# Drawing the first group's patch weights out of all experts by one-hot matmuls, with identity matmuls and four score banks in that group

## What is computed

```python
x = x + _L0_conv_ref(_gn(x), Wg, bg, Wexp, bexp)
x = x + _L1_conv_ref(_gn(x), w_route, b_route, w_experts)
x = x + _L2_conv_ref(_gn(x), codebook)
x = x + _L3_conv_ref(_gn(x), w_grid, b_grid, w_conv)
```

```python
feat = patched.mean(axis=(2, 3))
logits = feat @ Wg + bg
probs = jax.nn.softmax(logits, axis=-1)
routing = jax.nn.one_hot(jnp.argmax(logits, axis=-1), E) * probs
```

## Time and profile before

| | |
|---|---|
| median of 3 runs | 1939.35 us (1932.0 to 1942.69) |
| the profiled execution | 1936.7 us |
| its span, first to last instruction | 1934.9 us |
| TensorE busy | 1606.0 us, 83% |
| VectorE busy | 1449.0 us, 75% |
| ACT busy | 1099.4 us, 57% |
| POOL busy | 1210.8 us, 63% |
| mean granted TensorE clock | 0.933 |

### The profile page before, as it was taken

The page is one execution under the profiler, slowest core; times in us unless marked ns, Lnnn a source line. Parts: engine busy times, 40 slices in busy tenths (PEclk is TensorE's granted clock), DMA queues, the critical chain, the costliest instruction groups (busy, mean ns, idle before and its releaser), DMA issues.

```text
span 1934.9 us, 41692 instructions
## 1 busy us (share of the span) xinstructions
PE 1606.0 (83%) x15426; PEld 1298.9 (67%) x15426; DVE 1449.0 (75%) x2960; ACT 1099.4 (57%) x1499; POOL 1210.8 (63%) x1413
## 2 busy tenths in 40 slices
PE   0238648989988898888988998889988898988998
PEld 0112346668956787668956797668956797668998
DVE  3047637888779877888779878898779866897776
ACT  0001145657755675557656476557665575658986
POOL 4004236677657866678667766677567865678764
PEclk9995568999989998999989999999989998999999
DMA  7954685569856796569865697569965795225543
GB/s 141 215 118 116 149 196 171 151 176 238 214 149 182 192 230 188 148 167 236 223 164 159 193 237 209 148 169 232 225 170 172 191 230 163 77 81 165 149 143 85
DMA packets 294774, 336.85 MB, mean 174 GB/s; under 512 B 219601, under 2 KB 233937, under 8 KB 290349
## 3 DMA queue, kind: packets, MB, share of 16 engines
q1 hardware_dynamic: 240712, 228.88, 45.6%
q0 software_dynamic: 36336, 84.55, 18.6%
q10 hardware_dynamic: 17524, 20.75, 3.7%
HBM read 260.57 MB, written 60.09 MB: 166 GB/s over the span
## 4 chain that ended last, share of the span: by engine, by line
PE 43%; DMA 13%; DVE 10%; POOL 9%; SPq 8%; issue 6%; DVEq 6%; ACT 3%; ACTq 1%; POOLq 0%
PE bank L1308 22%; PE bank L1407 5%; DMA words<-in_codebook,code 4%; POOL fetched L600 4%; SPq L438 4%; PE bank L1295 4%; PE bank L1392 3%; POOL words L623 3%; DVE code L1184 3%; SPq L420 3%; PE bank L1365 3%; DVEq L1183 3%; DMA y_patches<-yc 2%; PE bank L1292 2%; DMA lent<-z_rows 2%
## 5 line engine op out<-in xcount | busy, mean ns | idle before, releaser
L600 POOL DMA_INDIRECT fetched<-row_pairs,corner x768 | 739.9, 963 | 425.6 <-DVE weighted L972 224.4
L1308 PE MATMUL bank<-lent,tent 128*128 128x160 f32 x6144 | 942.5, 309 | 1.2 <-issue 1.2
L1308 PEld LDWEIGHTS bank<-lent,tent 128*128 128x128 f32 x6144 | 877.4, 196 | 95.3 <-issue 69.3
L734 ACT ACTIVATE tent<-lent,row_at_sb 128x768 f32<-128x768 f32 x512 | 448.5, 923 | 61.4 <-PE bank L1308 42.6
L964 DVE TENSOR_TENSOR strip<-bank,near 128x480 f32<-128x480 f32 x512 | 332.3, 650 | 127.9 <-PE bank L1308 123.3
L738 ACT ACTIVATE tent<-tent 128x1536 f32<-128x1536 f32 x256 | 380.1, 1485 | 20.8 <-issue 0.4
L623 POOL DMA_INDIRECT words<-in_codebook,code x256 | 246.4, 962 | 118.6 <-DVE code L1184 66.5
L978 DVE TENSOR_REDUCE samp<-strip 128x96 f32<-128x480 f32 x414 | 270.3, 653 | 39.2 <-issue 1.8
L1407 PE MATMUL bank<-cb,xs 64*128 64x512 f32 x512 | 248.1, 720 | 35.2 <-DVE code L1184 18.1
L820 ACT COPY xs<-xn 32x128 f32<-32x128 f32 x256 | 75.6, 295 | 242.5 <-PE bank L1407 224.7
L1182 DVE MAX8 top<-bank 128x8 f32<-128x512 f32 x256 | 175.4, 685 | 45.0 <-PE bank L1407 44.9
(11 more groups left out here) (136 smaller groups left out, 1130.9 us busy)
## 6 DMA issues: line engine op xcount, KB each, us to landing
lent<-z_rows SPq DMA_DIRECT2D x256, 384.0 KB
picked_weights<-arena SPq DMA_DIRECT2D x14, 1800.0 KB
arena<-picked_weights SPq DMA_DIRECT2D x21, 720.0 KB
arena<-windows SPq DMA_DIRECT2D x288, 50.0 KB
arena<-xp SPq DMA_DIRECT2D x96, 136.0 KB
fetched<-row_pairs,corner POOLq DMA_INDIRECT x768
arena<-row_pairs SPq DMA_DIRECT2D x64, 160.0 KB
slice<-picked_weights SPq DMA_DIRECT2D x14, 720.0 KB
```

The lines of the kernel that those rows point to most:

```text
L600: pool.indirect_dma_start(fetched[:, N % FETCHES, k].rearrange("p q c -> p (q c)"), None, pairs_dram[b % 2], bass.IndirectOffsetOnAxis(ap= ...
L734: act.activation(w[:, piece], zs[:, N % SPREADS, :], ACT.Abs, bias=row_at[:, piece:piece + 1])
L1308: m = pe.matmul(STRIPS[j % 3][:, XW * C * e:XW * C * (e + 1)], tent[:, N % TENTS, c, DENSE * d + e], picture[:, b % 2, i, c], start=(c == ...
```

## The change

For group 0 alone the patch weights no longer go through DRAM. All eight experts' weights are loaded once (`every_expert`, 8 partitions x 3072, at partitions 0, 32 and 64 for the three kernel columns d). The expert of each patch is there as a one-hot column: the transposed `lg[:, 4]` is copied to `hot`, 8 x 100, three times. A matmul of the experts' weights for one output channel o (8 x 96) with `hot` gives the weights of all 100 patches for that o and d (96 x 100). `draw_weights` does this for 32 channels x 3 columns, in 8 steps of 4 channels, into two sets of three banks; `draw_first` on VectorE and on ACT copies each bank into the five patch rows' places; VectorE's has the same form as ACT's below, for the banks that ACT leaves. All five rows have a place of their own now (`first_xs`, `first_w`), so the five slices of windows (`load_first`, now on SP) wait only for the windows to be in DRAM.

Two more things change for group 0. `keep_running(n)` issues n matmuls of the identity with itself into a bank that nobody reads, at six places: 40 before the pooling matmul, 20 before the second convolution, 8 before the scores, 3 after each pair of scores, 6 and 14 around the last transpose of words. And the scores use four banks in place of two. `prepare` moves ahead of the copy of the features, and its last rows (`add_norms`) behind the drawing.

```diff
+STEPS = 8
+PIECE = C // STEPS
...
+        hot = sb("hot", [2 * C + E0, ITEMS])
...
-        first_picked = [tent[:].rearrange("p u c d n -> p (u c d n)")[0:ITEMS, 0:PICK],
-                        lent[0:ITEMS, STRUNG * 128:STRUNG * 128 + PICK]]
+        every_expert = tent[:].rearrange("p u c d n -> p (u c d n)")[:, 0:C * 3 * C]
...
+        DRAWN = [[P0, P1, P2], [P3, P5, P6]]
+        FIRST_SCORES = [P0, P1, P3, P5]
...
+        def drawn_by_act(j, d):
+            return d == 2 or (d == 1 and j % 2 == 1)
@@ SP @@
+            def load_first(v):
+                for i in range(IMG):
+                    if v == 0:
+                        sp.wait_ge(win_out[i], 16)
+                    a = win_dram[i].rearrange("(p c) s -> c p s", c=C)[:, NV * v:NV * (v + 1)]
+                    for dy in range(3):
+                        sp.dma_start(first_xs[v][C * dy:C * (dy + 1), i], a[:, :, dy * WIN:dy * WIN + CUT]
+                                     ).then_inc(first_in[v], 16)
...
             windows(0)
-            for v in range(SLICES):
-                load_slice(0, v)
+            for v in range(NV):
+                load_first(v)
@@ POOL @@
             windows(0)
-            for v in range(NV):
-                pick_first(v)
             for h in range(2):
                 clear_edges(h)
@@ ACT @@
+            def draw_first():
+                for i in range(IMG):
+                    act.wait_ge(win_out[i], 16)
+                for j in range(STEPS):
+                    act.wait_ge(drawn, j + 1)
+                    for d in range(3):
+                        if drawn_by_act(j, d):
+                            for v in (0, 1, 3, 4):
+                                m = act.copy(*draw(j, d, v))
+                            m.then_inc(drawn_act, 1)
...
-            for k in range(KEPT):
+            load_x(0)
+            for d in range(3):
+                act.dma_start(every_expert[C * d:C * d + E0], A["Wexp_t"][:, d]).then_inc(experts_in, 16)
+            for k in range(1, KEPT):
                 load_x(k)
@@ VectorE @@
-            dve.wait_ge(loaded, LOADS)
+            prepare()
             copy_features(0)
             route(0)
             gates(0)
+            dve.wait_ge(route_t, 1)
+            for d in range(3):
+                m = dve.tensor_copy(hot[C * d:C * d + E0, :], P4[0:E0, 256:256 + ITEMS])
+            m.then_inc(hot_ready, 1)
             copy_route(0)
             copy_gates(0)
-            prepare()
+            draw_first()
+            add_norms()
@@ TensorE @@
+            def draw_weights():
+                pe.wait_ge(experts_in, 16 * 3)
+                pe.wait_ge(hot_ready, 1)
+                for j in range(STEPS):
+                    if j >= 2:
+                        pe.wait_ge(drawn_dve, drawn_through(j - 2, False))
+                        pe.wait_ge(drawn_act, drawn_through(j - 2, True))
+                    for u in range(PIECE):
+                        for d in range(3):
+                            r = slice(C * d, C * d + E0)
+                            o = 3 * C * (PIECE * j + u)
+                            m = pe.matmul(DRAWN[j % 2][d][0:3 * C, ITEMS * u:ITEMS * (u + 1)],
+                                          every_expert[r, o:o + 3 * C], hot[r, :], start=True, stop=True)
+                    m.then_inc(drawn, 1)
...
+                def keep_running(n):
+                    if g == 0:
+                        for _ in range(n):
+                            pe.matmul(P6[:, 0:128], ident[:], ident[:], start=True, stop=True)
...
                     n = IMG * (TILES * g + t) + i
+                    banks = FIRST_SCORES if g == 0 else SCORES
                     pe.wait_ge(staged2, n + 1)
-                    if n >= 2:
-                        pe.wait_ge(score_read, n - 1)
+                    if n >= len(banks):
+                        pe.wait_ge(score_read, n + 1 - len(banks))
...
                             scores(t, i)
                             scores(t, i + 1)
+                            keep_running(3)
```

More of the change, by code:

```diff
@@ L206, in build @@
         w_out = sem("w_out")
-        first_named = sem("first_named")
+        experts_in = sem("experts_in")
+        hot_ready = sem("hot_ready")
+        drawn = sem("drawn")
+        drawn_dve = sem("drawn_dve")
+        drawn_act = sem("drawn_act")
         first_in = [sem(f"first_in{v}") for v in range(NV)]
-        first_out = [sem(f"first_out{v}") for v in range(NV)]
         wsum_ready = sem("wsum_ready")
@@ L320, in beside_score, with drawn_through, draw @@
             return SCORE_HALVES * n // (IMG * TILES), SCORE_HALVES * (n + 1) // (IMG * TILES)
+        def drawn_by_act(j, d):
+            return d == 2 or (d == 1 and j % 2 == 1)
+        def drawn_through(j, by_act):
+            return sum(drawn_by_act(n, d) == by_act for n in range(j + 1) for d in range(3))
+        def draw(j, d, v):
+            src = DRAWN[j % 2][d][0:3 * C, 0:PIECE * ITEMS].rearrange("p (o n) -> p n o", o=PIECE)
+            o = slice(PIECE * j, PIECE * (j + 1))
+            items = IMG * NV
+            if v == 1:
+                src = src[:, items:3 * items].rearrange("p (s n) o -> p s n o", s=2)
+                dst = arena[0:3 * C, 0:2 * SLICE].rearrange("p (s n) -> p s n", s=2)[:, :, XS:].rearrange(
+                    "p s (n d o) -> p s n d o", d=3, o=C)[:, :, :, d, o]
+            else:
+                src = src[:, items * v:items * (v + 1)]
+                dst = first_w[v].rearrange("p n i d o -> p (n i) d o")[:, :, d, o]
+            return dst, src
         MOST = (NV - 1) * NV
@@ L1049, in route @@
                 dve.drain()
-                if k == 1:
-                    for v in range(NV):
-                        dve.wait_ge(first_in[v], 16 * 2)
-                elif k > 1:
+                if k > 1:
                     for h in range(2):
@@ L1379, in front @@
                 at("pool")
+                keep_running(40)
                 pe.wait_ge(pooled, g + 1)
@@ L1402, in scores @@
                     n = IMG * (TILES * g + t) + i
+                    banks = FIRST_SCORES if g == 0 else SCORES
                     pe.wait_ge(staged2, n + 1)
-                    if n >= 2:
-                        pe.wait_ge(score_read, n - 1)
+                    if n >= len(banks):
+                        pe.wait_ge(score_read, n + 1 - len(banks))
                     half = slice(2 * C * (i % 2), 2 * C * (i % 2 + 1))
-                    pe.matmul(SCORES[n % 2][:, :], xs2[half, i // 2, :], cb2[half, :], start=True, stop=True
+                    pe.matmul(banks[n % len(banks)][:, :], xs2[half, i // 2, :], cb2[half, :], start=True, stop=True
                               ).then_inc(score_done, 1)
@@ L1518 @@
         "Wexp": a["L0_conv_Wexp"].transpose(0, 3, 2, 4, 1).reshape(2 * E0, PICK),
+        "Wexp_t": a["L0_conv_Wexp"].transpose(0, 4, 1, 3, 2).reshape(E0, 3, C * 3 * C),
         "bexp": a["L0_conv_bexp"],
```

118 lines of the change are left out of this document (58 added, 60 removed).

## The result

The changed kernel takes 1873.95 us, the median of four runs (1868.04 to 1880.16); the kernel before took 1935.67 us as the median of four (1930.3 to 1942.69). The ratio is 0.9675, with a 95% interval of 0.9639 to 0.9711. The prediction was 1872 us in a range of 1858 to 1896. The profiled execution took 1873.85 us, with a span of 1872.0.

A forecast was written before the change was run, and what follows sets the result against it. It took the program as one serial line until the first picture load, with gather, store and reload delaying weights and slices. Terms -49, -2.8, -12 and -2.4 sum to -66.2 from 1936.7, giving 1870.5, set at 1872 us; range 1858 to 1896.

The forecast's parts named there:

- Part 1: Group 0's weights: drawing replaces gather, store and reload, so the last convolution ends at 60, not 108.9: -49 us.
- My dear end, 0.61: Slow end for group 0's slices: 0.61 us per command from 26, last convolution ending at 72.6, term -36.
- third rival: Gather was hidden anyway: the slices' pace is their own, over 1 us per command; 1921 us, chance 0.04.
- the drawing was no bound: Rival on the drawing matmuls: triples run one after another, 44 us, making the drawing the bound; 1897 us, chance 0.09.
- Part 2: Up to the second convolution: identity matmuls cost nothing and raise the clock, so its first half is faster: -2.8 us.
- slower* rival: All 136 identity matmuls come on the path at the low clock, 68 us outweighing the 49: 1957 us, chance 0.02.
- Part 3: Score stage: four banks let matmuls run while VectorE reads the pair before, so VectorE sets the pace: -12 us.
- Part 4: Behind the scores: with the clock up, offset matmuls take half of 3.69 and transposes a little less: -2.4 us.
- first rival: Clock isn't held in the scores: a low pair costs TensorE 4.05 us, four banks help nothing; 1888 or 1894, chance 0.22.
- The "some 6" us: Before the picture load: SP's last slice command, with 12 us to spare before the change, keeps some 6.
- Behind the picture load: From the first picture load to the end: the work is the same row for row, so no change, 0.

The follow-up runs named there:

- e4: The kernel before, with identity matmuls and four score banks added but without the drawing of weights: 1932.57 us, ratio 0.9964.
- e1: The changed kernel with the drawing alone, two score banks and no identity matmuls: 1878.47 us, ratio 0.9702.
- e10: e7 with group 1's weight gathers issued ahead of the scores and their stores behind the stacking of rows: 1884.27 us, ratio 0.9733.
- e7: The changed kernel with group 0's looked-up words transposed three tiles of scores later, not two: 1866.69 us, ratio 0.9640.
- e8: The changed kernel with POOL's picture-border writes held back until group 0's fourth slice has landed: 1870.32 us, ratio 0.9670.
- e11: e7 without any identity matmul: 1872.47 us, ratio 0.9674.
- e2: The changed kernel without identity matmuls but with four score banks: 1875.87 us, ratio 0.9663.
- e12: e7 with the SBUF tiles moved back to their addresses before the change: 1873.59 us, ratio 0.9675.

## Why the prediction was right, and where it was not

**What bounds the kernel.** "The program is one serial line until the first picture load" held in the main: e4 and e1, which move the load by 6.7 and 44.8, shorten the time by some 4 and 58, and e10, which puts it 13.4 us later than e7, costs 17.6. But the forecast sum was one for the picture load, and there it was 13.3 us short: -52.9 for -66.2, the load at 181.96 for the 169 forecast. The end came out at -62.9 because of 10 us that stand in no part of the prediction. That is luck.

**Part 1, -49, measured -45.9.** The main step held: with gather, store and reload gone the weights are ready at 40 and the slices are the last to come. Two sizes were off, in this order of events. The read of the features starts late: the store of the window means is 5.43 us long on the chain (12.77 to 18.20), and only 2.68 in e4, which doesn't draw. The border writes aren't the cause, since it takes 5.66 in e8, which holds them back. The three loads of all experts, new on ACT's queue ahead of most of the input, differ too; that they are the cause was not tried. The late read moved the one-hot columns from the forecast 22.3 to 25.1. The slices still start at 22.67, where I took 24. What cost time was the slices' pace, 0.59 us for the 0.47 taken: 60 x 0.12 = 7.2 later, of which the earlier start gave back 1.3 and a landing within 1.5 us, for the 4 taken, 2.5. My dear end, 0.61, covers it, and the third rival's pace, over 1 us, did not come. For the matmuls without a row I took 0.46 us for three at once; they took 3 x 0.125 = 0.37, and the drawing was no bound.

**Part 2, -2.8, measured -2.8.** The second convolution takes 5.36 us (7.97 before), all of it at a granted clock of 1.00, behind sixty identities. e11 gives the counter-test: 7.78 without. The identities before it cost nothing, since TensorE idled 6.11 and 1.22 us behind them. That settles the *slower* rival for this kernel: outside the score stage none of its identities ends on the path, and in it they cost 0.3 us by the stages of the changed kernel and e2, 1.5 by those of e7 and e11. In e7, where the last words come at another time, six of them do stand on the path.

**Part 3, -12, measured -4.7. This step failed.** The arithmetic of banks was right: pairs take 2.9 us, and where hardly a score waits for words the stage takes 53.2, 52.1 and 51.8 us (e7, e12, e11), where the forecast had 52. VectorE's waits for scores are what differs between the kernels: 13.7 us before, 9.8 in the changed kernel and in e2, 3.8 in e7 and e10; the rest of the stage is 49 to 51 us in all five. What failed is the sentence "the chain gather, store, slice load is the next to be late, and not yet". It was late at once, in two ways. One I had not looked at: the look-ups share POOL's queue with the gather and the DMA engines with the store. Before the change the pairs were 3.8 us apart and that left the words time (TensorE waited once, 3.9 us, behind the last score). With pairs of 2.9 it waits four times, 13.7 us in all. I had the gather at 182.04 in the earlier trace rows and asked when it comes, not who stands behind it. The other way is that of Part 4. e10 shows that little else was missing: with gather, store and reload out of the way, and the words three tiles late, first score to picture load takes 72.3 us, and Parts 3 and 4 make it 52.2 + 19.4 = 71.6.

The first rival, that the clock isn't held, described the first pair well: at a granted clock of 0.50 (102 to 106 us) a pair with identities takes 4.00 us, for 4.05 forecast. The Trainium skill (TensorEngine Tiling (Array Packing), key properties of the tiling modes) says that TensorE drains when the tiling mode changes. The 4.00 agrees with parts that add up, and no run here shows the drain by itself. But the rival's conclusion fell: it made the low clock decide the stage. The clock did not hold at 1.00 up to the offsets, as I forecast, and the stage is shorter all the same. In e2 the clock is lower still and the stage as long, since without identities a low pair takes 2.3 us of TensorE. In the first pair the identities made the load that they were to remedy.

**Part 4, -2.4, measured +0.4.** The offsets take 2.02 us for 3.69, as forecast. Then the row-pair store takes 5.45 us on the chain, which had this before:

```profile
232.31 2.57 DMA row_pairs<-pairs
```

Group 1's slices (SP, 159.84 to 174.0) come late against a front that is early, and their last command loads 720 KB of weights:

```profile
173.58 0.44 SPq L481 DMA_DIRECT2D arena<-picked_weights  x1
```

In the eight kernels in which this command ends 2 to 5 us ahead of the store, the store takes 3.6 to 6.2 us and lands 7.7 to 8.5 us behind that end; in the six in which over 9 us lie between, e10 among them, it takes 2.5 to 2.6. So the picture load hangs on the weights' load too. The "some 6" us that I had left to spare counted the command and not its landing.

**Behind the picture load, 0, measured -10.** Not forecast. With moved addresses the 256-byte packets are faster, which is shown; that the 10 us come from the move is likely by the medians above, but the three tests give 2 to 13 us with intervals of about the same size, and what waits for these packets was not found. The rest may be scatter between executions. So the total was as near as 2 us by luck: this gain stood in for most of the 13.3 missing at the picture load, 7.3 in the scores, 2.8 behind them and 3.1 in the weights.

## What to carry to other kernels

Ask of every large transfer not only when it starts but which small ones stand behind it on its queue or beside it on the DMA engines, and what waits for those in order; when the compute ahead of them gets faster, that wait appears. Where a stage has the same length under different clocks and edits, look for what paces it from outside. An in-order engine can be freed of a late load by asking for it one step later, but follow the chain on: in e7 the stage lost 6.3 us and the picture load only 2.4, since the wait moved behind the stage. Moving the transfer to an emptier-looking stretch can cost more (e10, 18 us over e7).

## What the runs showed that I had not expected

- Gathers of 100 rows (1.8 MB each) make what is near them wait: beside two of them the first layer's rows landed after 21.29 us instead of 3.48, and a look-up behind one after 10.64, where the last look-up took 2.44.
- Thin matmuls on separate row groups are cheap: 8 rows x 96 columns with 100 columns of `hot` take 0.125 us each in triples.
- The address of tiles in SBUF matters for DMA: with the large tiles 360 bytes further on, 256-byte packets take 17.7 to 17.8 ns and not 19.4 to 19.6, with the same packets on the same queue.
